# A DLRM interaction tower on one Trainium2 core: another order of the steps, Gram copies on ScalarE in batch 0, low table parts from PSUM

## What is computed

```python
e = jnp.stack([tbl_0[ids[:, 0]], ..., tbl_25[ids[:, 25]]], axis=1)     # 2048 x 26 x 128
combined = jnp.concatenate([e, r_dense_x[:, None, :]], axis=1)          # 2048 x 27 x 128
interact = jnp.einsum('bfd,bgd->bfg', combined, combined)
z = interact[:, _TRIU_I, _TRIU_J]                                       # 2048 x 351 pairs
h = jnp.concatenate([z, r_dense_x], axis=1)                             # 2048 x 479
h = jnp.maximum(h @ W_top1 + b_top1, 0.0)                               # 512
h = jnp.maximum(h @ W_top2 + b_top2, 0.0)                               # 256
y = h @ W_top3                                                          # 2048 x 1
```

## Time and profile before

| what | value |
|---|---|
| median of 3 runs | 392.79 us (390.19 to 393.61) |
| the profiled execution's own time | 390.99 us |
| its span, first to last instruction | 388.9 us |
| PE matmul busy | 329.5 us, 85% |
| POOL busy | 277.6 us, 71% |
| DVE busy | 233.4 us, 60% |
| ACT busy | 178.4 us, 46% |
| granted TensorE clock, mean | 0.974 of full speed |

### The profile page before, as it was taken

How to read it: one execution, slowest core, us unless ns; L and a number is a source line. 1 busy time by engine, 2 the same in 40 slices (tenths; PEclk the granted TensorE clock), 3 DMA queues, 4 the chain that set the end, 5 groups by cost and what they waited for, 6 DMA issues and landing times.

```text
span 388.9 us, 11971 instructions
## 1 busy us (share of the span) xinstructions
PE 329.5 (85%) x5327; PEld 238.8 (61%) x5327; DVE 233.4 (60%) x380; ACT 178.4 (46%) x263; POOL 277.6 (71%) x288
## 2 busy tenths in 40 slices
PE   4987898758658898979899898989899699989766
PEld 3666676546546655556767655566677445568655
DVE  6897899558835956638797946647786303032030
ACT  5463554434422525444553615444454645465523
POOL 7888777777777777777777777777777777777300
PEclk9999998969979999999999999998999999999999
DMA  7996153333333332333334332333311211222000
GB/s 190 257 267 178 54 123 86 84 83 81 78 82 85 82 77 56 83 110 82 79 83 111 84 78 55 85 108 83 78 54 56 57 52 53 57 56 57 28 4 2
DMA packets 24194, 33.60 MB, mean 86 GB/s; under 512 B 6527, under 2 KB 17538, under 8 KB 24144
## 3 DMA queue, kind: packets, MB, share of 16 engines
q0 software_dynamic: 8960, 18.37, 17.1%
q1 hardware_dynamic: 15184, 14.48, 15.8%
HBM read 32.82 MB, written 0.01 MB: 84 GB/s over the span
## 4 chain that ended last, share of the span: by engine, by line
POOL 51%; PE 25%; issue 20%; ACT 2%; DMA 2%; POOLq 0%; ACTq 0%
POOL gat L366 49%; PE prod L425 5%; PE prod L427 5%; PE gram L453 4%; PE back L494 3%; PE back L498 2%; PE front L399 2%; POOL oh_last L372 2%; PE back L484 1%; DMA oh_last<-in_tbl,idx 1%; ACT ct L584 1%; DMA gat<-in_tbl,idx 1%; PE gram L498 1%; ACT h L609 1%; PE back L479 0%
## 5 line engine op out<-in xcount | busy, mean ns | idle before, releaser
L366 POOL DMA_INDIRECT gat<-in_tbl,idx x272 | 267.6, 984 | 83.0 <-issue 82.4
L685 DVE TENSOR_SCALAR ring<-idb,rowid 125x516 fp32r<-125x516 int32 x216 | 146.6, 742 | 27.7 <-PE prod L427 27.0
L425 PE MATMUL prod<-ring,tab_hi 125*128 125x512 f32 x264 | 109.6, 415 | 4.5 <-ACT oh_last L563 2.1
L427 PE MATMUL prod<-ring,tab_lo 125*128 125x512 f32 x264 | 106.3, 403 | 0.0
L584 ACT COPY ct<-front 128x512 f32<-128x512 f32 (+2 forms) x80 | 73.0, 965 | 36.5 <-PE front L399 32.7
L692 DVE COPY z<-gram 128x216 f32<-128x216 f32 x32 | 12.2, 382 | 107.5 <-PE gram L453 107.5
L453 PE MATMUL gram<-ct 128*27 128x27 f32 x4096 | 55.5, 194 | 18.0 <-issue 10.0
L453 PEld LDWEIGHTS gram<-ct 128*27 128x27 f32 x4096 | 45.8, 104 | 35.4 <-issue 27.9
L425 PEld LDWEIGHTS prod<-ring,tab_hi 125*128 125x128 f32 x264 | 51.4, 195 | 18.6 <-issue 3.8
L399 PE MATMUL front<-ident,gat 128*128 128x128 f32 x272 | 44.4, 290 | 20.5 <-DMA gat<-in_tbl,idx 12.7
L427 PEld LDWEIGHTS prod<-ring,tab_lo 125*128 125x128 f32 x264 | 51.2, 194 | 10.4
(11 more groups left out here) (72 smaller groups left out, 211.2 us busy)
## 6 DMA issues: line engine op xcount, KB each, us to landing
idb<-in_ids_t SPq DMA_DIRECT2D x27, 258.0 KB, 4.1
gat<-in_tbl,idx POOLq DMA_INDIRECT x272
oh<-in_tbl SPq DMA_DIRECT2D x3, 448.0 KB
oh<-in_dense_t SPq DMA_DIRECT2D x4, 256.0 KB, 3.2
gat<-in_tbl SPq DMA_DIRECT2D x2, 448.0 KB
h<-in_tbl SPq DMA_DIRECT2D x2, 448.0 KB
w1z<-in_w SPq DMA_DIRECT2D x1, 702.0 KB
w2s<-in_w SPq DMA_DIRECT2D x1, 512.0 KB
```

The source lines that it names most:

```text
L366: nc.gpsimd.indirect_dma_start(out=gat[:, t % GS, i, :], out_offset=None, in_=tables[GATHERED[i]][:, :], in_offset=bass.IndirectOffsetOnAx ...
L425: nc.tensor.matmul(prod[:, :], tab_hi[0:OH_P, m, k, :], ring[0:OH_P, k, 0:SB], start=(k == 0), stop=False)
L427: nc.tensor.matmul(prod[:, :], tab_lo[0:OH_P, m, k, :], ring[0:OH_P, k, 0:SB], start=False, stop=(k == OH_K - 1)).then_inc(used, 1)
L685: nc.vector.tensor_scalar(ring[0:OH_P, k, :], idb[0:OH_P, n % IDB, :, 0:IW], rowid[0:OH_P, k:k + 1], None, ALU.is_equal).then_inc(built, 1)
```

## The change

**Order.** `tile_steps` is rewritten. Placing is now a step of its own tile, behind the turn, in most tiles (in the third tile of a batch, the next one's is still between the Gram chunks). Batch 0 gets one one-hot field in tile 0, two in tile 1, four in tile 2 and two in tile 3. The last two layer blocks of job 1 move from tile 11 to tile 12; those of job 2 move by about one place. In the last tile all of the half job stands ahead of the last fill; nothing of it is left behind Gram. Layer 3 of the last jobs uses the bank `prod`.

```diff
-        return (... + A[6:7] + [("P", 0)] + O[0:1] + G[0:1] + PL + G[1:2] + O[1:2] + G[2:4])
+        return (... + A[6:7] + PT + O[0:1] + G)
     if t == TILES - 1:
-        return T[0:1] + N[4:5] + T[1:2] + N[5:6] + T[2:3] + Z + T[3:4] + N[6:7] + E[0:4] + T[4:5] + G + E[4:7]
+        return (T[0:1] + N[4:6] + T[1:2] + Z + PT + E[0:4] + T[2:3] + N[6:7] + E[4:6] + T[3:4] + E[6:7] + T[4:5] + G)
     if last and u == 0:
-        return T[0:2] + J[0:0] + T[2:4] + Z + T[4:5] + J[0:2] + G[0:1] + PL + G[1:2] + J[2:3] + G[2:4]
+        K = L(b - 2)
+        return T[0:2] + K[5:6] + T[2:3] + Z + T[3:4] + K[6:7] + PT + T[4:5] + J[0:2] + G
     if last and u == 1:
-        return T[0:2] + J[3:4] + T[2:3] + Z + T[3:5] + J[4:5] + G[0:1] + PL + G[1:2] + J[5:6] + G[2:4]
+        return T[0:2] + J[2:3] + T[2:3] + J[3:4] + T[3:4] + Z + PT + T[4:5] + J[4:5] + G
     if last:
-        return T[0:2] + J[6:7] + T[2:3] + Z + T[3:5] + N[0:2] + G[0:1] + PL + G[1:2] + N[2:4] + G[2:4]
+        return T[0:2] + J[5:6] + T[2:3] + Z + T[3:4] + J[6:7] + PT + N[0:2] + T[4:5] + N[2:4] + G
+    if b == 0 and u == 1:
+        return T[0:2] + O[1:2] + Z + T[2:3] + PT + O[2:3] + T[3:5] + G
+    if b == 0 and u == 2:
+        return T[0:2] + O[3:4] + Z + T[2:3] + PT + O[4:5] + T[3:5] + G[0:1] + PN + G[1:2] + O[5:6] + G[2:4] + O[6:7]
+    if b == 0:
+        return T[0:2] + O[7:8] + Z + T[2:3] + O[8:9] + T[3:5] + G
...
+    if b + 2 == NB:
+        return T[0:2] + O[7:8] + Z + T[2:4] + O[8:9] + T[4:5] + G
...
-    return step[0] == "L" and step[1] >= NB - 2 and step[3] % 2 == 1
+    return step[0] == "L" and step[1] >= NB - 2 and (step[3] % 2 == 1 or step[2] == 3)
```

```diff
 def ahead_of(t):
-    if t + 1 == TILES or not onehots_of(t + 1):
-        return 0, 0, 0, 0
-    steps = [s for s in tile_steps(t) if s[0] in "GO"]
-    return (0, 6, 0, 0) if steps[-3][0] == "O" else (2, 1, 2, 1)
+    return {0: OH_K, 1: OH_K, 2: 4, 3: 4}[t % BT] if t >= BT else OH_K
+def scalar_copies(t, c):
+    return t < BT or c % 2 == 0
```

```diff
-        def fill_columns(c):
-            return range(c * TCH, min((c + 1) * TCH, NG))
+        def fill_columns(t, c):
+            part = (c + TF - 1) % TF if t < BT else c
+            return range(part * TCH, min((part + 1) * TCH, NG))
         def extra(t, c):
-            return NX if t < BT and c == TF - 1 else 0
+            return NX if t < BT and c == 0 else 0
```

```diff
+            def copy_halves(m):
+                act.wait_ge(table_in[m], 32)
+                if m > 0:
+                    act.wait_ge(lo_ready, m)
+                for h in range(2):
+                    nc.scalar.copy(table_half(h), raw_table(m)[:, h * SB:(h + 1) * SB]).then_inc(halves_copied, 1)
...
             def split_low(m):
                 dve.wait_ge(hi_ready, m + 1)
-                nc.vector.tensor_sub(tab_lo[0:OH_P, m, :, :]..., raw_table(m), tab_hi[0:OH_P, m, :, :]...).then_inc(lo_ready, 1)
+                for h in range(2):
+                    dve.wait_ge(halves_copied, 2 * m + h + 1)
+                    rows = slice(h * OH_K // 2, (h + 1) * OH_K // 2)
+                    ins = nc.vector.tensor_sub(tab_lo[0:OH_P, m, rows, :]..., table_half(h), tab_hi[0:OH_P, m, rows, :]...)
+                ins.then_inc(lo_ready, 1)
```

**Gram weights.** The stationary operand takes the 5 padding columns (zeros) with it:

```diff
-                        one = ct[:, t % 2, c * CG + i, j, 0:NF]
-                        ins = nc.tensor.matmul(gram_bank(n)[QUAD * j:QUAD * j + NF, i, :], one, one, start=True, stop=True)
+                        one = ct[:, t % 2, c * CG + i, j, :]
+                        ins = nc.tensor.matmul(gram_bank(n)[QUAD * j:QUAD * (j + 1), i, :], one, one[:, 0:NF], start=True, stop=True)
```

More of the change, by code:

```diff
@@ L259, in gathers_landed @@
         def gathers_landed(t, c):
-            return sum(len(fill_columns(c)) + extra(i, c) for i in range(t % GS, t + 1, GS))
+            return sum(len(fill_columns(i, c)) + extra(i, c) for i in range(t % GS, t + 1, GS))
         def raw_table(m):
@@ L369, in gather @@
                         ).then_inc(gathered[t % GS][c], 16)
-                if t < BT:
-                    for e, f in enumerate(ONEHOT[NA:]):
+                    for e, f in enumerate(ONEHOT[NA:NA + extra(t, c)]):
                         nc.gpsimd.indirect_dma_start(
@@ L605, in finish_block @@
                     h, bias = ((h1, b1s), (h2, b2s))[n - 1]
-                    if (n, m) == (1, 0) and 0 < job < NB:
+                    if (n, m) == (2, 0) and 0 < job < NB:
                         act.wait_ge(y_out, 16 * job)
@@ L649, in _ @@
                         if tuple(q) == (0, NA - 1):
-                            for m in range(NA, NO):
-                                split_high(m)
+                            for m in range(NA + 1, NO):
+                                copy_halves(m)
                     elif kind == "P":
                         place_columns(*q)
-                    elif kind == "G" and q[1] % 2 == 0:
+                    elif kind == "G" and scalar_copies(*q):
                         copy_gram(*q)
@@ L719, in build, with build_some @@
                     build_chunk(b, m, k)
+            def build_some(fields, lo, hi):
+                for field in fields:
+                    build(field, lo, hi)
             build(("O", 0, 0), 0, OH_K)
@@ L725, in _ @@
                 build(("O", 0, m), 0, OH_K)
+            for m in range(NA, NO):
+                split_low(m)
             made = 0
@@ L728, in _ @@
                 fields = onehots_of(t)
-                if t > 0 and not (t % BT == 0 and fields):
+                late_pick = t > BT and t % BT == 0 and fields
+                if t > 0 and not late_pick:
                     pick_pairs(t - 1)
@@ L732, in _ @@
                     build(fields[0], made, OH_K)
-                if t > 0 and t % BT == 0 and fields:
+                if late_pick:
                     pick_pairs(t - 1)
-                if t == 0:
-                    for m in range(NA, NO):
-                        split_low(m)
-                for field in fields[1:]:
+                after = fields[-1:] if t % BT == 2 else []
+                for field in fields[1:len(fields) - len(after)]:
                     build(field, 0, OH_K)
-                made = 0
+                first = after or onehots_of(t + 1)[0:1]
+                made = ahead_of(t) if first else 0
+                if t % BT != 2 or t < BT:
+                    build_some(first, 0, made)
                 for c in range(GC):
-                    if c % 2:
+                    if not scalar_copies(t, c):
                         copy_gram(t, c)
-                    if ahead_of(t)[c]:
-                        build(onehots_of(t + 1)[0], made, made + ahead_of(t)[c])
-                    made += ahead_of(t)[c]
+                    if t % BT == 2 and t >= BT and c == 1:
+                        build_some(first, 0, made)
+                if after:
+                    build(after[0], made, OH_K)
+                    first = onehots_of(t + 1)[0:1]
+                    made = 0
             pick_pairs(TILES - 1)
```

81 lines of the change are left out of this document (49 added, 32 removed).

## The result

| | before | after |
|---|---|---|
| median | 392.12 us (390.19 to 393.61) | 399.84 us (398.21 to 400.53) |
| profiled execution, span | 390.99, 388.9 | 399.94, 398.1 |
| PE busy | 329.5 | 338.7 |
| GpSimd busy | 277.6 | 271.0 |
| mean granted clock | 0.974 | 0.961 |

The changed kernel takes 1.019 times as long [1.014, 1.025] as the one before: slower, clear of the noise, by about 2%. I had forecast 386 us, and "slower" with a chance of 0.06. (Times are medians; the brackets behind a ratio are its 95% interval. "Before" is timed again beside each group of experiments, and each ratio is to that.)

A forecast was written before the change was run, and what follows sets the result against it. GpSimd's gathers were taken as the bound, PE close behind. Span 388.9 less 7.1 (gathers), +2.7 and −2.7 (tail), +1.2 (additions) gave 383.0, so 386 us; own range 382 to 389.5, with rivals 377.5 to 391.5.

The forecast's parts named there:

- Steady tiles: Tiles between batch 0 and tile 14: same work in other places, PE waits for rows in tile 14; cost 0.
- Batch 0: Reordered first four tiles: tile 3's Gram ends near 112 us instead of 129.2; worth nothing itself, buys slack.
- Splits from PSUM: Low parts read from PSUM stop holding gathers: gathers 7.1 us earlier, last issue at 355.8; bounds 0 and 10.9.
- Tiles 14 and 15: End of the kernel: Gram of tile 14 done at 349.2, last transposes at 365.6, then 16.2 us, plus 1.2 additions.
- rival 1: Tile 15: the half job doesn't hold the last fill; last transposes at 358.5, time 377 to 379; chance 0.14.
- Rivals 1 and 2: The second: splits still hold gathers, or denser gathers lose as much beside float builds; time 391 to 393; chance 0.14.
- Rival 4: Batch 0 doesn't come forward because ScalarE's copies of halves hold the splits; time near 390; chance 0.10.
- Rival 3: Gram products: weight loads bound them, 1.15 us more a tile over 15 tiles; time 398; chance 0.05.
- theory D: From the experiments, not the prediction: GpSimd's gather issues hold the engines' instruction supply, whatever they run; no chance given.

The follow-up runs named there:

- e3: Changed kernel with the order of the kernel before from tile 4 on; new batch 0, PSUM splits, fills and wide weights kept: 387.0 us, 0.983.
- e9: Changed kernel with every second Gram group of each chunk left out, so half the Gram products aren't computed: 383.4 us, 0.972.
- e2: Changed kernel with a product or layer block moved between Gram chunks 1 and 2 in nine more tiles: 390.5 us, 0.994.
- e12: Kernel before, in its own order, with only the low parts read from PSUM and 32-column Gram weights: 388.0 us, 0.983.
- e1: Changed kernel with the Gram weights back at 27 columns: 401.8 us, 1.024.
- e10: e3 with a step between Gram chunks 1 and 2 in tile 0 and every tile from 4 on with one to spare: 384.7 us, 0.976.
- e11: Kernel before with the step between Gram chunks 1 and 2 put ahead of Gram in tiles 0, 12, 13 and 14: 394.4 us, 1.000.
- e5 to e8: Same kernels as e11, e9, e10 and e12, when everything ran slowed: 663.8, 664.3, 710.7 and 678.9 us; the kernel before took 670.1.
- e6: Same kernel as e9 (changed kernel, half the Gram products left out), when everything ran slowed: 664.3 us.
- e5: Same kernel as e11 (kernel before, step put ahead of Gram in four tiles), when everything ran slowed: 663.8 us.

## Why the prediction was wrong

**Steady tiles: the step that failed.** "The same work in other places ... Cost 0, hidden by the gathers." Tiles 4 to 14 took 13.6 us more. I had PE at the end of tile 13 at 324.7, 17 us earlier than before and so waiting for rows in tile 14; its pairs were there for VectorE at 342.6, 0.9 later than before. Two things were wrong in it. First, I counted a step's cost as the sum of its instructions' durations, as if their place didn't matter, where the place of one 4 us step decides whether 512 short instructions follow one another; the trace of before had it in view, in "35.4 <-issue 27.9" for Gram's loads, and I read that row for its 104 ns only. Second, I took slack for given. The gathers can hide PE's losses only while PE waits for them, and in these tiles it didn't: before, it took 87.1 us for four tiles whose gathers take 85, and between batch 0 and tile 15 it never waited for rows. The slack in my sum was what batch 0 was to come forward, 17 us, some 6 of it to spare. It came forward by 9.1, and tiles 4 to 14 took 13.6 more.

What is shown of the cause: e3 gives 12.8 us back with the old order, so the loss is the new order's. e9 (no gaps with half the instructions, every wait still in place) shows that the gaps come from runs of short instructions, and e2 (the same work with Gram cut in two) that they cost time where PE bounds, 9.3 us. What isn't shown is how the 13.6 divide. The stalls on "issue" grew by only 3.4 us in these tiles, and e2 takes away nearly all of Gram's 12.4, those that the kernel before had too. The lower clock is an estimated 5.6 more, and the waits for ScalarE and VectorE are 4.2 more. No run takes these waits away alone.

**Batch 0: right in sign, half the size.** Tile 3's Gram was to end at 112 and ended at 120.1 (129.2 before). Waits of 5.1 us for builds in batch 0 (3.3 and 1.8) and the gaps of tiles 0, 1 and 3 (5.5 us) weren't in the sum.

**Splits from PSUM: right in the cause, less in the end time.** No gather is held by a split any more: beside one none takes over 1.19 us, where before they took up to 2.59. The mean fell from 984 to 958 ns, which over 272 is 7.1 us, as I had it (964 ns and 5.4 us in e12, where a gather of 2.47 us ahead of a split remains). The last issue was to come at 355.8: it came at 357.72 in e12 and at 360.03 in the kernel after, where GpSimd waited 5.1 us for PE. A split is 1.29 us for two of 512 columns (I had 1.4). The Trainium skill ("SBUF — State Buffer", "Who interferes with whom") has it that a VectorE instruction with at most one SBUF input, outside the 2-port modes, doesn't contend with GpSimd: this trace agrees, by 16.10 us of the timeline above, where a gather takes 0.94 beside a split.

**Tiles 14 and 15.** From Gram(14), the end of tile 14's Gram, to the last transposes I had 16.4 us, by waits of each block for the one before; it took 14.7 (361.6 to 376.27, the last transposes' start). They stand 13.7 us behind the last rows' landing (360.03 + 2.5), where I had said 7: the half job does hold them, as forecast, against rival 1, and PE's lateness comes on top. The tail's order costs by itself: from the end of tile 14's Gram to that of tile 15's e2 takes 21.2 us (351.6 to 372.8; 2.6 of it gaps), the kernel before 16.6 (0.2 of it gaps, 1.9 a wait for rows). Behind the last transposes I had 16.2 + 1.2; it took 21.8:

```profile
376.27 0.33 PE L423 MATMUL front<-ident,gat 128*128 128x128 f32 x1
377.32 1.18 PE L482 MATMUL gram<-ct 128*32 128x27 f32 x112 [0.72 <-ACT ct L623]
379.58 1.34 PE L482 MATMUL gram<-ct 128*32 128x27 f32 x128 [1.08 <-issue]
383.03 0.33 PE L482 MATMUL gram<-ct 128*32 128x27 f32 x16 [2.11 <-issue]
...
388.05 2.93 PE L524 MATMUL front<-zt,w1z 117*128 117x128 f32 x12 [0.57 <-ACT zt L638]
```

Between the first and last of these rows 3.2 us are two gaps in the last Gram run; 1.7 are the lower clock behind them (0.77 in that stretch: line 524's 24 matmuls take 4.68 us and took 2.94). The turn did come right behind the pairs (386.49, behind 386.44), which is why the stretch behind Gram(15) is 0.5 shorter all the same.

**Terms together.** 383.0 was forecast, 398.1 came: +12.4 up to Gram(14) (361.6 for 349.2), -1.7 up to the last transposes, +4.4 behind them.

**The rivals.** Rivals 1 and 2 fell with what stands above. Rival 4 half came: batch 0 came forward, by 9.1 of 17 us. Rival 3 had the right side and 398 us, and the wrong mechanism: wider weights cost 5 to 6 ns a load, but e1 shows that the Gram run doesn't wait for it. (By the columns over 1.2 ns of the Trainium skill, "TensorE: Matmul & The Clock Gate", LDWEIGHTS, five columns are an estimate of 4.2 ns; the rows of e1, 105 against 110 ns, agree with its size.) What it had in view, that small matmuls are heavy on issue, was the right place to look, for the supply of instructions and not for the weight path.

## What to carry to other kernels

Instructions come in packets, and a run of short ones can be through before the next packet is there: here 512 of them in 4 us stalled TensorE for 0.8 to 3.2 us, and the same work with a 4 us step in its middle stalled for more than half a microsecond in one case only (e10). So spread short instructions between long ones. An "issue" wait of an engine that has its inputs is a row to explain, not noise, and where two engines run within 1 us a tile of each other, as here, freeing one makes the gaps of the other count. A change with a gain in one part and another order in the rest should be timed apart: here one was worth -1.7%, and the rest of the change cost 3.7% on top (1.019 over 0.983).

## What the runs showed of the hardware

**Instruction packets.** 16 KB, 256 instructions of PE, never closer than 3.25 us; when PE had run dry it went on 1.2 to 1.6 us behind the end of a packet's transfer (141.06 to 142.42 after; in e11 358.22 to 359.73). The prediction has no term for it. What sets off the fetch of a packet, and whether it could come earlier, wasn't tried.

**The clock behind a gap.** The kernel after has five issue gaps of more than 2 us, and a stretch at 1.2 instead of 2.4 GHz begins in or within 2 us behind each of them (at 57.2, 77.7, 142.6, 234.7 and 384.9). The last 14.7 us were granted 0.77 of full speed, 1.00 before. Ahead of the last of these stretches PE also began a wait of 2.04 us for the pairs (at 384.4), so there the two causes aren't told apart; in e2 the clock fell at 371.6, inside the gap.

**Stalls while gathers are issued (e5 to e8).** In these four PE's time was lost in one place. A row of PE's timeline of e6, and two of its list of waits:

```profile
317.52 0.27 PE L487 MATMUL gram<-ct 128*32 128x27 f32 x4 [0.49 <-issue]
```

```profile
POOL gat L392 <- PE front L424: 234.6, 13, 24.2
PE gram L487 <- issue: 221.0, 227, 2.6
```

While a tile's 17 gathers were being issued (from 310.53 to 331.43 for the tile of this row), PE got through a handful of pairs or fewer per 0.7 to 2.1 us. Its 16 long matmuls of lines 450 and 452 in the same stretch ran at 0.4 us each, as usual; outside of it the pairs did too, and GpSimd then waited for PE. Half the Gram instructions (e6) left 227 gaps of 221 us, against 225 of 222 in e5: there the number of instructions didn't count, and 227 gaps are far more than the 26 packets, so these aren't the gaps of the other runs. This is the picture that theory D had. The cause isn't known.
